# The end of phase 1 placed among the first two tiles of expert 0, in a fused attention and mixture-of-experts kernel

## The reference

```
h    = rmsnorm(layernorm(x)) * gamma
q, kv, a = split(h @ w_qkva.T); a = sigmoid(a)
y_t  = a_t * y_(t-1) + kv_t             # along the 1024 tokens
x1   = x + q * y
n    = layernorm(x1)                    # rows of the second half
top-2 experts of 8 by softmax(n @ router); a position in each expert's
list by a running count over the group's tokens; at most 256 per group and expert
out  = x1 + sum over a token's two experts of gate * (gelu(n @ w0) * (n @ w1)) @ wo
```

## Time and profile before

| | |
|---|---|
| median of 3 runs | 1752.66 us (1750.37 to 1752.7) |
| the profiled execution's own time | 1755.55 us |
| its span in the profile | 1753.8 us |
| PE busy | 1693.2 us (97%) |
| DVE, ACT, POOL busy | 833.6, 713.8, 388.6 us |
| mean granted TensorE clock | 0.977 of full |

### The profile page before, as it was taken

How to read it: one execution, slowest core, us unless ns; L and a number is a source line. 1 busy time by engine, 2 the same in 40 slices (tenths; PEclk the granted TensorE clock), 3 DMA queues, 4 the chain that set the end, 5 groups by cost and what they waited for, 6 DMA issues and landing times.

```text
span 1753.8 us, 25482 instructions
## 1 busy us (share of the span) xinstructions
PE 1693.2 (97%) x10284; PEld 1514.3 (86%) x10284; DVE 833.6 (48%) x1672; ACT 713.8 (41%) x1236; POOL 388.6 (22%) x310
## 2 busy tenths in 40 slices
PE   5989996999999999999999999999999999999997
PEld 4778885989999988899899899899899989989886
DVE  5888875333533354335433453345334533353332
ACT  4556552333533343334433443344333433353332
POOL 3366756411011111111111111111111111111111
PEclk9988986999999999999999999999999999999999
DMA  9356533211411151115111421132113311241111
GB/s 310 131 170 214 194 104 134 59 25 22 116 26 24 25 121 25 25 25 113 33 25 25 97 49 25 25 88 58 25 25 74 72 25 25 53 93 16 34 13 13
DMA packets 112318, 120.76 MB, mean 69 GB/s; under 512 B 14472, under 2 KB 99912, under 8 KB 112200
## 3 DMA queue, kind: packets, MB, share of 16 engines
q1 hardware_dynamic: 87624, 85.29, 16.3%
q0 software_dynamic: 24576, 33.83, 11.3%
HBM read 59.84 MB, written 59.24 MB: 68 GB/s over the span
## 4 chain that ended last, share of the span: by engine, by line
PE 87%; DVE 4%; POOL 4%; ACT 2%; issue 2%; DMA 1%; SPq 0%; POOLq 0%; ACTq 0%
PE bank L1156 53%; PE bank L1172 28%; PE bank L1020 3%; POOL slots L522 2%; PE bank L1096 2%; DVE y L783 1%; POOL pw L506 1%; PE bank L1066 1%; DVE st L803 0%; DVE z L789 0%; PE bank L1056 0%; ACT x2nT L619 0%; POOL sc L510 0%; POOL out L571 0%; ACT xn L594 0%
## 5 line engine op out<-in xcount | busy, mean ns | idle before, releaser
L981 DVE TENSOR_TENSOR y<-bank,sig 128x512 f32<-128x512 f32 (+1 forms) x352 | 243.3, 691 | 571.1 <-PE bank L1156 561.2
L571 POOL DMA_INDIRECT out<-xring x128 | 200.9, 1569 | 1221.4 <-ACT xring L726 1189.8
L709 ACT ACTIVATE hhi<-y 128x512 fp32r<-128x512 f32 (+1 forms) x352 | 222.3, 631 | 525.4 <-DVE y L981 525.4
L1156 PE MATMUL bank<-xThi,whi 128*128 128x512 f32 x1408 | 426.1, 383 | 0.0
L1156 PE MATMUL bank<-xTlo,whi 128*128 128x512 f32 x1408 | 425.4, 382 | 0.0
L1156 PE MATMUL bank<-xThi,wlo 128*128 128x512 f32 x1408 | 423.8, 381 | 0.0
L1172 PE MATMUL bank<-whi,hhi 128*128 128x256 f32 (+1 forms) x1408 | 389.7, 277 | 0.0
L1172 PE MATMUL bank<-wlo,hhi 128*128 128x256 f32 (+1 forms) x1408 | 387.8, 275 | 0.0
L1172 PE MATMUL bank<-whi,hlo 128*128 128x256 f32 (+1 forms) x1408 | 387.4, 275 | 0.0
L984 DVE TENSOR_TENSOR hlo<-y,hhi 128x512 fp32r<-128x512 f32 (+1 forms) x352 | 243.6, 692 | 245.6 <-ACT hhi L709 245.6
L703 ACT ACTIVATE sig<-bank 128x512 f32<-128x512 f32 (+1 forms) x352 | 209.3, 595 | 289.8 <-PE bank L1156 289.8
(11 more groups left out here) (110 smaller groups left out, 1072.0 us busy)
## 6 DMA issues: line engine op xcount, KB each, us to landing
stage<-in_L_ffn_w_kernel SPq DMA_DIRECT2D x160, 128.0 KB, 3.0
slots<-fill SPq DMA_DIRECT2D x32, 520.0 KB, 6.1
xring<-slots SPq DMA_DIRECT2D x32, 520.0 KB, 3.5
stage<-in_L_ffn_wo_kernel SPq DMA_DIRECT2D x80, 128.0 KB, 3.0
xring<-in_L_attn_x SPq DMA_DIRECT2D x16, 512.0 KB, 4.4
out<-xring SPq DMA_DIRECT2D x16, 512.0 KB, 4.1
slots<-rows,sloti POOLq DMA_INDIRECT x128
out<-xring POOLq DMA_INDIRECT x128, 3.8
```

Source lines behind the costliest of these rows:

```text
L571: pool.indirect_dma_start(out_rows, bass.IndirectOffsetOnAxis(idx, 0), ysb[:, t % 2, j, :], None, compute_op=ALU.add).then_inc(added, 16)
L709: act.activation(hhi[0:n, hc % 3, :], hf[0:n, hc % 2, :], ACT.Copy).then_inc(h_hi, 1)
L981: dve.tensor_tensor(hf[0:n, hc % 2, :], up[hc % 2][1][0:n, :], gel[0:n, hc % 2, :], ALU.mult).then_inc(mul_done, 1)
L1156: last = pe.matmul(lines(up[hc % 2][w][:, :]), (whi, wlo)[wp][:, hc, at:at + P], lines((xThi, xTlo)[xp][:, t % 2, k, :]), start=m == 0 and ...
```

## The change

The last group's tail and the routing of the last two groups are no longer done in turns 8 and 9, but as pieces behind chunks of tiles 0 and 1 of expert 0 (`drain` on PE, ACT and DVE). Six things go with it.

1. **Rows first.** SP asks for the rows of tiles 0 and 1 before the last two stores of x1, not behind them. PE transposes tile 0's first half behind the last projection and its second half behind `transpose2` of group 6.
2. **The drain.** PE gets `transpose_back` of group 7 at (0,1) and (0,3), `count` of group 6 at (0,3), `transpose2` at (0,7) and (0,9), `route` at (0,8) and (0,10), and `count` of group 7 at (1,2). DVE and ACT get their pieces in the same chunks.
3. **Banks.** The up projections have one bank for gate (bank 2), so that each gate waits for the gelu of the chunk before. Value has bank 3 alone in tile 0, and banks 3 and 5 in turn afterwards. The transposes of `prepare` have one bank in place of two.
4. **prepare** is split in two, behind chunks 5 and 7 in place of chunk 6, in every tile.
5. **POOL** scatters group 6 during tile 0, and group 7 behind tile 0's four output DMAs.
6. ACT's wait for the x1 stores moves from the gelu of (0,0) to the end of tile 0.

```diff
-PREPARE = 6
+PREPARE = (5, 7)
...
-        up = [bank[2:4], bank[5:7]]
-        yb = [bank[4], bank[7]]
+        tr = bank[0]
+        up_gate = bank[2]
+        yb = [bank[4], bank[1]]
+        def up_value(e, t, hc):
+            return bank[3] if hc % 2 == 0 or (e, t) == (0, 0) else bank[5]
...
             load_rows(0, 0)
+            load_rows(0, 1)
+            step(Turn(G))
...
+            powers2(last_group, 0)
+            scatter(before_last, 0, HT)
+            powers2(last_group, 1)
+            end_scatter(before_last, 0)
+            scatter(before_last, HT, TILES)
+            end_scatter(before_last, 1)
...
+                    if (e, t) == (0, 0):
+                        scatter(last_group, 0, TILES)
...
             def up_chunk(e, t, hc):
...
-                user = c - 2 if hc >= 2 else c - hc - HC + max(q for q in range(HC) if q % 2 == hc)
+                if e + t + hc > 0:
+                    pe.wait_ge(gelu_done, HC * FT * e + c)
...
+                if (e, t) == (0, 0):
+                    user = c - 1
                 pe.wait_ge(mul_done, HC * FT * e + user + 1 + FREE_MUL)
```

More of the change, by code:

```diff
@@ L428, in _ @@
             slots_are_empty(Turn(FT - 1))
-            for i in range(G - 2, G + 1):
+            for i in range(G - 2, G):
                 step(Turn(i))
@@ L709, in expert @@
                         act.activation(hhi[0:n, hc % 3, :], hf[0:n, hc % 2, :], ACT.Copy).then_inc(h_hi, 1)
[L710 to L711 removed]
+                        if hc in PREPARE and (t < FT - 1 or not last):
+                            prepare(*(e, t + 1) if t < FT - 1 else (e + 1, 0), PREPARE.index(hc))
+                        if e == 0:
+                            drain(t, hc)
                         if fetch and hc >= 3:
@@ L962, in step, with drain @@
                     statistics1(i.plus(2), 1)
-            pipeline(dve, step)
+                if i.value == G - 1:
+                    prepare(0, 0, 0)
+                    prepare(0, 0, 1)
+                    shift(before_last)
+            pipeline(step)
+            def drain(t, hc):
+                if (t, hc) == (0, 1):
+                    softmax(before_last)
+                    choose(before_last, 0)
+                if (t, hc) == (0, 2):
+                    choose(before_last, 1)
+                    residual(last_group, 0)
+                if (t, hc) == (0, 3):
+                    statistics2(last_group, 0)
+                if (t, hc) == (0, 4):
+                    place(before_last)
+                if (t, hc) == (0, 5):
+                    factors2(last_group, 0)
+                    residual(last_group, 1)
+                if (t, hc) == (0, 6):
+                    statistics2(last_group, 1)
+                if (t, hc) == (0, 7):
+                    factors2(last_group, 1)
+                if (t, hc) == (0, 10):
+                    shift(last_group)
+                if (t, hc) == (1, 0):
+                    softmax(last_group)
+                if (t, hc) == (1, 1):
+                    choose(last_group, 0)
+                    choose(last_group, 1)
+                if (t, hc) == (1, 3):
+                    place(last_group)
             def next_weights(e, hc):
@@ L1088, in _, with prepare @@
             last.then_inc(wq_t, 1)
-            def prepare(e, t):
+            def prepare(e, t, k):
                 p = t % 2
[L1093 to L1097, removed]
+                if k == 0:
+                    pe.wait_ge(rows_loaded[p], 16 * FT // 2 * e + 16 * (t // 2 + 1))
+                else:
+                    pe.wait_ge(fx_lo, KD * FT * e + KD * t + k)
+                for j in range(FJ):
+                    last = pe.transpose(tr[:, j * P:(j + 1) * P], rows2[:, p, j, k * P:(k + 1) * P], ident[:, :])
+                last.then_inc(ft, 1)
             def step(i):
@@ L1184, in expert @@
                         up_chunk(e, t, hc)
-                        if hc == PREPARE and (t < FT - 1 or not last):
-                            prepare(*(e, t + 1) if t < FT - 1 else (e + 1, 0))
+                        if hc in PREPARE and (t < FT - 1 or not last):
+                            prepare(*(e, t + 1) if t < FT - 1 else (e + 1, 0), PREPARE.index(hc))
+                        if e == 0:
+                            drain(t, hc)
                         if hc >= 2:
```

139 lines of the change are left out of this document (94 added, 45 removed).

## The result

The changed kernel took 1745.16 us (median of 18 runs, 1743.33 to 1750.32) and the kernel before 1752.18 us beside it (18 runs, 1750.37 to 1755.53). The ratio is 0.9963, with a 95% interval of 0.9956 to 0.9969: 7.0 us faster, against 7.0 forecast and a time of 1745.7.

What follows compares the result with a forecast made beforehand. PE was taken to bound the kernel, with 36.1 us nearly idle between phases. Of 128.0 us, 103.8 work and 8.1 waits leave 16.0; less 5.3 clock, 2.8 gate bank and 0.9 split, 7.0 gained: 1745.7 us, range 1743 to 1749.

Steps and rivals of the forecast that it cites:

- The moved work: Pieces moved into tiles 0 and 1: transposes 5.3 us, three `route` 5.9, two `count` 2.2; with two tiles, 103.8.
- Start: Before tile 0's first chunks: PE waits 0.9 us for copies of transposes and 0.3 at gate (0,1) for gelu, 1.2.
- (0,3): Tile 0, chunk 3: `transpose_back` waits 1.8 us for DVE's residual.
- gate (1,2): Tile 1, chunk 2: with one bank, gate waits 2.4 us for gelu (1,1), behind two table loads and the exp.
- (1,2) again: Same chunk: `count` of group 7 waits 2.3 us for the masks from DVE.
- The clock: Low clock stretches from the projections to tile 2 cost 5.3 us: 0.9 at the start plus two and a half times 1.76.
- the clock stays up: Rival: after the start, waits of at most 2.4 us don't lower the clock; 4.4 us more gained, 1741.3 us; chance 0.17.
- it falls at every piece: Rival: the clock falls at every moved piece, costing 12.3 us in place of 5.3; 1752.7 us; chance 0.20.
- The gate's wait in every tile: Rival: PE needs the gelu's semaphore well before gate, so every tile pays; with 1 us lead about 1763 us; chance 0.08.
- Rows that come late: Rival, tile 0: its rows share DMA engines with store and scatter and delay the start by 5 us; 1751; chance 0.05.
- What stays in every tile: One gate bank costs 0.4 us at seven expert starts, 2.8 (2.4 to 4.2); the split of `prepare` costs 0.9 in 31 tiles.
- The table loads: Tile 1, chunk 1: by the skill's drain rule two switches cost 2.8 us more, leaving a gain of 4.2 us.

Runs made afterwards that it cites:

- the second series: Four follow-up kernels, one an unedited copy of the changed kernel, measured when the kernel before took 1753.12 us; that copy was 9.4 us faster.
- Run 3: Changed kernel with `prepare` whole again behind chunk 6, with two transpose banks, outside tiles 0 and 1: 1776.54 us, ratio 0.9944 to the kernel before.
- runs 2 and 6: Changed kernel with group 7's exp moved to tile 0's end, 1776.6 us; and with that, two gate banks and whole `prepare` together, 1740.22 us.
- the control: Changed kernel again with no edit but a blank line: 1743.76 us, ratio 0.9949 to the kernel before.
- runs 3 and 7: Changed kernel with `prepare` whole behind chunk 6, 1776.54 us; and with `transpose_back` and both `count` pieces one chunk later, 1739.85 us.
- run 4: Kernel before with one gate bank and nothing else of the change: 1792.57 us, ratio 1.0042 to the kernel before.
- run 1: Changed kernel with two gate banks, bank 6 taking odd chunks outside tile 0: 1774.34 us, ratio 0.9939 to the kernel before.
- the first series: Four follow-up kernels measured when the kernel before took 1783.54 us, 31 more; no unedited copy of the changed kernel ran there.

## Why the prediction was right, and where it was off

**The place and the sign.** The argument that PE alone sets the end, that 36 us pass nearly idle at the seam, and that the change is worth this time less moved work and new waits, held: 116.8 us to tile 2 against 117.3 forecast. That the median came out at just the 7.0 forecast is in part luck: the terms below miss both ways, and the second series has 9.4.

**The moved work.** It fits the tiles' lengths. Tile 1, 51.20 us, is a plain tile of 45.2, a `count` of 1.1, the waits of 2.3 and 0.4, and 2.2 for the low clock. Tile 0, 59.69 us, is 45.2, about 8.2 of moved pieces (four groups of transposes at 0.87, two `route` at 1.8, `count`), a wait of 1.4, 2.9 of low clock at its start, and 1.9 at (0,3): 59.6. The 2.2 is what tile 1 leaves over; from the gate of (1,2) at 327.3 to `count` at 332.2 the starts show 1.8 of it.

**The waits.** The places were right but for one: none was seen at (0,7), for which I had 0.4. Start 1.6 (forecast 1.2), (0,3) 1.4 (1.8), gate (1,2) 2.3 (2.4). *(1,2) again* is the term that was most mis-sized: 0.4 measured, 2.3 forecast. I had set DVE's path against PE's at full clock. But the low clock behind the gate's wait stretched PE's work until the masks were nearly done. The one loss covered the other. Run 3 shows it on the same code: with the clock at full behind the gate's wait of 2.3, the masks' wait is 2.0. With the gelu's wait gone it is 2.3 and 2.6, in runs 2 and 6. A sum that adds waits and low stretches as if they were independent counts such a pair twice.

Two terms of this sum weren't worked out right. At the start, two copies of 0.6 to 0.7 less a cover of 0.89 come to 0.3 to 0.5, not 0.9, and the row shows 1.6. What was left out is that DVE still had the last projection's scan and product (`y`, `z`) ahead of its copy: ACT's copy ended at 255.4, DVE's began at 256.4. And gate (0,1) doesn't wait for gelu (0,0), for which I had 0.3: PE's work ahead of it ran at the low clock and covered it. At (0,3), 9.3 less 7.6 is 1.7, not 1.8.

**The clock.** 5.3 forecast; what is left of 116.8 after 103.8 of work and 5.7 of waits is 7.3. The start cost 2.9 where I had 0.9. I had taken one stretch's 1.76 and let half of it vanish under the waits there, but the low stretch hid only gate (0,1)'s 0.3 and came behind the wait of 1.6, and the low level held over 18 up matmuls, which took 6.9 us where the earlier trace rows has 5.74 for 18. Two more cost 1.9 and 2.2, a little over the 1.76 priced, where I had two and a half. The errors of the waits (-2.4) and the clock (+2.0) cancel, so this total is better than its terms.

**The rivals.** That the clock stays up fell with the stretches at 0.72, though at (0,3) it did stay up in the control, and behind the gelu's wait in runs 3 and 7. That it falls at every piece fell with 1.00 at both `route` in dense work. The gate's wait in every tile fell with tiles of 45.21 to 45.26, and run 4. Rows that come late, and a change that doesn't do what it says, fell too: PE never waits for a DMA in the drain, and gate (0,0) starts 5.7 us behind the last projection, about the 5 forecast.

**What stays in every tile.** The step that one gate bank costs 0.4 at each of seven starts was mis-sized: it is 0.6 (4.1 us in run 1, 4.2 in run 4), the upper bound that I had given. I worked out the idle time, and the row shows it at 0.31. But the gate behind it also takes 1.58 instead of 1.32, which no wait view counts. The split came out at 0.8 for 0.9.

**The table loads.** In (1,1) of the changed kernel the chain shows both switches:

```profile
323.14 0.55 ACT hhi L737
...
323.78 1.28 ACT L639
325.08 0.26 ACT ex L639
325.35 1.28 ACT L731
326.64 0.61 ACT sig L731
```

The loads take 1.28 each, and the exp starts 0.02 and the gelu 0.01 behind them. The drain of about 1.38 us that the Trainium skill has in "ScalarE: Activation LUTs", "What ACT_TABLE_LOAD costs", isn't there: the gap ahead of the first load is 0.09 and ahead of the second 0.01. The wait that hangs on it was 2.3, where the rows gave 2.4 and the rule some 2.8 more. Here the measurement decides.

**What stays open.** Why the first series took 31 us more. The record has the same chip number for both series, so that another chip is the cause isn't shown. PE, ACT and DVE were idle there with "issue" named as releaser, in phase 1's end and in tiles 0 and 1, as in run 3:

```profile
PE bank L1265 <- issue: 6.5, 2, 6.2
```

Nothing that was run tells what they waited for. Open too is why the clock falls behind the gelu's wait of 2.3 us in two executions (the changed kernel and its copy) and not in runs 3 and 7.

## What to carry to other kernels

Filling a seam between two phases with dense work pays, but place each moved piece by when its producer is done, on its engine's queue, and not by order alone: one chunk later for three pieces gave 3.9 us here, beside 9.4 for the whole change in the same series. Waits in a row hide each other, so remove the whole row: in tile 1, 0.9 and 2.1 us apart, 4.7 together. Before a bank is given up, look at the slack in the tightest tile, not the usual one, and price a wait by the distance between starts, not by its idle row.

## What the runs showed of the hardware

- A wait of 2.3 us in otherwise dense work needn't lower TensorE's clock, and can. Behind the same wait of gate (1,2) it stayed at 1.00 in runs 3 and 7, and fell in the changed kernel (0.53 over 327 to 330) and in its copy (0.71 over 330 to 335).
- The small matmuls of `count` weren't what lowered it at (1,2): in the changed kernel the low stretch comes ahead of `count`, at which the clock was full (1.00 over 332 to 334). In its copy the clock was full there too (1.00 over 333 to 335). In run 3 it fell behind `count` (0.66 over 359 to 364). Nor did `route` between dense chunks lower it (1.00 at 300 to 305 and 310 to 315).
- At (0,3) the same code fell in one execution (0.72) and not in another (1.00), after the same 1.4 us wait. One profile doesn't settle such a place.
- A group of six matmuls behind a wait of 0.31 us took 1.58 us instead of 1.32, so the tile got 0.6 longer.
